# A four-layer megakernel: the order of all engines' steps written out anew

## What is computed

```python
x = L0_attn_x
xn = _layernorm(x, axis=-1)
s = _L0_attn_ref(xn, ...)          # rotary + Mamba-2 style chunked state space mixer
g = _silu(_L0_ffn_ref(xn, ...))    # gated MLP, inputs and weights quantized to FP4 in blocks of 16
x = x + s * g
xn = _layernorm(x, axis=-1)
s = _L1_attn_ref(xn, ...)          # attention over 16 heads within a token, 1.5-entmax by sorting
g = _silu(_L1_ffn_ref(xn, ...))    # mixture of 8 experts, top 2
x = x + s * g
xn = _layernorm(x, axis=-1)
s = _L2_attn_ref(xn, ...)          # gated delta rule: a recurrence over all tokens, rotated state
g = _silu(_L2_ffn_ref(xn, ...))    # mixture of 8 experts, top 2, with a shared expert
x = x + s * g
xn = _layernorm(x, axis=-1)
s = _L3_attn_ref(xn, ...)          # causal attention, 16 heads, relative positions by a skew
g = _silu(_L3_ffn_ref(xn, ...))    # gated MLP, integer weights
x = x + s * g
```

## Time and profile before

| | us |
|---|---|
| median of three runs | 3212.63 |
| the three runs | 3210.42, 3212.63, 3227.47 |
| span of the profiled execution | 3209.0 |
| layers 0 to 2, with the loads ahead of them | 0 to 1951 |
| layer 2's outputs | 1951 to 2233 |
| layer 3: preparation, attention, feed-forward | 2233 to 2300, to 3110, to 3209 |
| table loads on ACT | 94 |

### The profile page before, as it was taken

The page is one execution under the profiler, slowest core; times in us unless marked ns, Lnnn a source line. Parts: engine busy times, 40 slices in busy tenths (PEclk is TensorE's granted clock), DMA queues, the critical chain, the costliest instruction groups (busy, mean ns, idle before and its releaser), DMA issues.

```text
span 3209.0 us, 40003 instructions
## 1 busy us (share of the span) xinstructions
PE 2383.4 (74%) x13729; PEld 1300.2 (41%) x13729; DVE 2544.2 (79%) x5554; ACT 1633.2 (51%) x3182; POOL 565.8 (18%) x610
## 2 busy tenths in 40 slices
PE   3697876967958769679674304997688898888888
PEld 1333333333333333334331101332366676666663
DVE  3386898998999999989989673887577777777764
ACT  1344436245344353353442412666587888777862
POOL 0000300302203003012030020001332323323320
PEclk9698987977978879779777655999799999999999
DMA  2001100100101001001010004200688877888751
GB/s 73 1 22 43 30 25 28 35 32 23 34 29 30 26 24 33 28 27 31 30 24 23 23 8 123 57 9 31 198 226 223 235 222 225 220 215 227 220 157 43
DMA packets 270758, 265.92 MB, mean 83 GB/s; under 512 B 15224, under 2 KB 244235, under 8 KB 268987
## 3 DMA queue, kind: packets, MB, share of 16 engines
q1 hardware_dynamic: 270554, 263.37, 28.8%
HBM read 130.48 MB, written 124.45 MB: 79 GB/s over the span
## 4 chain that ended last, share of the span: by engine, by line
DVE 41%; PE 31%; ACT 14%; issue 9%; DMA 2%; POOL 2%; SPq 1%; DVEq 0%; POOLq 0%; ACTq 0%
PE banks L2642 5%; PE banks L2688 4%; DVE t L2618 3%; DVE t L1017 2%; PE banks L2602 2%; DVE t L1169 2%; ACT L144 2%; DVE t L952 1%; ACT t L2629 1%; PE banks L1085 1%; ACT t L2553 1%; DVE t L2673 1%; DVE t L1700 1%; DVE t L1704 1%; ACT t L1395 1%
## 5 line engine op out<-in xcount | busy, mean ns | idle before, releaser
L2618 DVE CUSTOM_DVE_ANT_0 t<-banks,t 128x640 f32<-128x640 f32 (+7 forms) x512 | 377.8, 747 | 135.2 <-PE banks L2642 62.2
L2629 ACT ACTIVATE t<-t 128x640 f32<-128x640 f32 (+7 forms) x512 | 391.0, 780 | 81.3 <-DVE t L2618 80.4
L2642 PE MATMUL banks<-ident,t 128*128 128x128 f32 x2304 | 360.1, 281 | 41.6 <-DVE t L2839 14.4
L2642 PEld LDWEIGHTS banks<-ident,t 128*128 128x128 f32 x2304 | 253.8, 142 | 108.1 <-ACT t L2629 50.5
L2602 PE MATMUL banks<-t 128*128 128x512 bf16 (+3 forms) x768 | 197.3, 333 | 39.4 <-DVE t L2618 37.5
L2583 POOL TENSOR_TENSOR t<-t 128x512 f32<-128x512 f32 x96 | 122.6, 1277 | 551.1 <-DMA t<-relative_scratch 455.7
L548 POOL TENSOR_TENSOR t<-t 128x512 f32<-128x512 f32 x28 | 48.1, 1718 | 915.7 <-ACT t L520 915.7
L2673 DVE COPY t<-banks 128x512 f32<-128x512 f32 x256 | 175.6, 686 | 32.2 <-PE banks L2642 31.3
L1085 PE MATMUL banks<-t 128*128 128x512 f32 x256 | 145.0, 650 | 42.9 <-DVE t L1165 32.3
L1740 ACT ACTIVATE t<-t 128x16 f32<-128x16 f32 x256 | 82.5, 322 | 184.1 <-DVE t L1704 142.4
L1119 ACT ACTIVATE t<-banks 128x512 f32<-128x512 f32 x128 | 76.4, 597 | 195.6 <-PE banks L1085 195.4
(11 more groups left out here) (453 smaller groups left out, 5956.2 us busy)
## 6 DMA issues: line engine op xcount, KB each, us to landing
relative_scratch<-t SPq DMA_DIRECT2D x128, 512.0 KB, 3.6
t<-relative_scratch SPq DMA_DIRECT2D x128, 512.0 KB, 5.2
relative_scratch<-t SPq DMA_DIRECT2D x128, 256.0 KB, 4.1
t<-in_wmoe SPq DMA_DIRECT2D x64, 384.0 KB, 3.0
t<-cut_scratch SPq DMA_DIRECT2D x192, 64.0 KB
t<-t SPq DMA_DIRECT2D x16, 512.0 KB, 4.2
cut_scratch<-t SPq DMA_DIRECT2D x8, 768.0 KB, 4.1
z_scratch<-t SPq DMA_DIRECT2D x8, 512.0 KB, 3.1
```

The lines of the kernel that those rows point to most:

```text
L2618: nc.vector.tensor_tensor_reduce(s.s[z][:, 0:n], ps[:, b0:b0 + 1 + i // 4, :].rearrange("p b n -> p (b n)")[:, 0:n], s.bias[r][:, j, WIDE ...
L2629: nc.scalar.activation(s.s[z][:, 0:n], s.s[z][:, 0:n], ACT.Exp, scale=-1.0, bias=s.least[:, z:z + 1]).then_inc(*a.mark("weights", u))
L2642: nc.tensor.transpose(ps[:, 4 + c % 2, (t - lo) * P:(t - lo + 1) * P], s.s[u % NS][:, t * P:(t + 1) * P], k.ident[:]).then_inc(*e.mark("tu ...
```

## The change

Ten strings of letters are replaced, nothing else. Each new string has the same number of each letter as the old one (TURNS_SP has one q less, which issued nothing). So every part issues its instructions in its own order as before; what differs is which part's step stands next to which on an engine. The new strings of layers 0 to 2 don't repeat from round to round, and those of the attention don't either. The core of the diff (lines of 112 letters):

```diff
 TURNS_PE = (
...
-    "ammmmmmmiimimmiimmiimmmmmmimimimimmmmeeettttttettmegegmaeeaeeeeaeeeeaeeeaefeeeeeemeeeemfefffeffeffeefeemeeemeeee"
...
+    "miiiimmmmmimmmmmmiimmimmmmmmmmttmmmmmttmteemtteetmgegeaaeaeeaeaeefmeeeefeffeefeeffeeffeeefeeeeffffeefeeeeeeeebee"
...
 )
 TURNS_ACT = (
...
-    "meeetttttgtgtgteggekmkmmeaeaeeaaefemeemfffffeemameeffeemmamaffmmefiebebaammmmrmmrarrirrimirimrmriirriririirrirrr"
...
+    "mmeetttttetteggtgggemkekmmaeaaeafmmmmeffeffffffffiebaeeeeemmaaeemeaaemmemmmbammmiiiiiiiiiimmimiiiirrriririririir"
...
 )
 TURNS_DVE = (
...
-    "afaafafefararaeafaefarafarfeffarfafafefefafefafeffefafafmefmafefmefmafmrrmamrmeiarbeebabararrmammamamramrarmrmra"
...
-    "rrrrrrrrrrrrrrrrrrrrrrrrrrrrrrrrrrrrrrrrrrrrrrrrrrrrrrrrrrrrrrrrrrrrrrrrrrrrrrrrrririririririiiiigiiiigigggggggg"
...
+    "afeeaafffffffffffffffffffffeaeeaaiaaeaeaeaaeaaeaeaeaaeeaaeamreeraaaaaraaaaaaaammrrrmmrmmmrrrmrrmmmrmmrrrmrrrrmmm"
...
+    "rrrrrrrrrrrrrrrrrrrrrrrrrrrrrrrrrrrrrrrrrrrrrrrrrrrrrrrrrrrrrrrrrrrrrrrrrrrrrrrrrrrrrrrrrrrrrrrriiirrrrggggggggg"
...
 )
 TURNS_SP = (
-    "bwtixqxwwqxxqqwwwwwwwwxxiiitqtwwwwwwwwxxiiittqwwwwwwwwbxxiiittqwwwwwwwwbxxiiittqqwwwwwwwwbxxiiittwwwwwwwwbxiiitt"
...
+    "twixbqqwwxxxqqwwwwwwwwxxiiittqwwwwwwwwxxiiittqwwwwwwwwbxxiiittqwwwwwwwwbxxiiittqwwwwwwwwbxxiiittwwwwwwwwbxiiittw"
...
 )
 TURNS3_DVE = (
-    "rabrrrrrrrrrrrrraaaabababababbbrrbaarbabrrrrrbrarararbrbbaaaabbbbaaababbbaaababbbaaababbbaaababbbaaababbbaababba"
...
+    "arbrrrrrrrrrrrrrbbbbbbbbaaaaaaababrbrbbaarbarrrrrbaababbraaababbbaaababbbaaabbabbraaababbbaaababbbaaababbraarabr"
...
 )
 TURNS4_PE = (
-    "vtsvssvvvvvvsttsssttssttttstvttsvtsvttsvsstvtsstvttsttvttsvvtstvtssstvtsstvtttvsttvttvsstvtstsstvsttsvttsvttvtsv"
...
+    "vstvvvssvvvvsttsssttsstttstttvttsstvtsvttssvvsstvttsttvttsvtvsttvssstvtssttvttsvttvtstvsttsvttsvsttvssttsvttvtst"
...
 )
 TURNS4_DVE = (
-    "vtsssstststststssvtvsstsvtvstststssvtvsstststvsvtstsstvvstsststvsvtststvsvsststvsvtststsstvsvstststvsvtstsstsvtv"
...
+    "vtsssstststststsstsvvtstsvvstststssvtvsstststvsvtstsstsvvtstssvtsvtstsstsvvtstsststsvvtsstsstvvstststvvssttssstv"
...
 )
```

More of the change, by code:

```diff
@@ L1821 @@
[L1821 to L1822 removed]
+    "aigefmbtmmmfmmfmffmffmffmffmmffmmmmmmffmmmmfmmmmmmmmmmmmmmmmmmeememaeaamaafeeeeeeeeefeeeffeeeeeeeefeemeeeeeeemee"
+    "eemffeffefeeeemeeeemeeeemmeffeemmmmmmmmffmmfeeeaaeeeaemmmmmmmmammiiimmmmmmmmiiiimmmmmmmmimmimimmimmmeemettetttte"
+    "tteeemgegeeeaaeaeaeaeeeefmffffffffffffffeeeeeeemeeeemeeemeeeeemeemeeeeeeeeeeaeeeeeeeaeeemmeaammmmmmmmmmiiimmmmmm"
@@ new lines @@
+    "mmbmammiiiriiririrmrmriimrmimmirmrrririrrirmiririrrirerirrrrrrrrrrreeiimmgggttttggtgttggtekkemammaaeaefffefffeff"
+    "fffieebeeaemmmaameeaaeeeemmememmrrrrrrrrmrmrmrbarimririirmrmrrrriirmmririririmirrrririririmmiimmiiiimmgggmmemmee"
+    "ggtttttegttggtekmkeaeaaafmmeeffefffemmffmmffmmfimemaebmeeaameeaaemebmeeeaiiiiiimiiiiimiimiiiiiiriimgmrrrrrrrrrrr"
+    "rrrrrrrrrrrrrrrrrrrrggmmmmmmmttggtttegteeggttikekeaaaeaebeeeeeeeeeeaeeeaabeaaeaiiiiiiiiiiiiiirirririrririrrrrrrr"
+    "rrrrrrrrrrrrrrrrrrgggiittttggtgtggttkkbbrrrrrrrrrrrrrrrrrrrrrrrrrrrrrrrrbb"
@@ new lines @@
+    "efmaeaeeaaaeaeaeaaaaeaaaaeeaaeafaafaefaeffffffaaeaaafeefmmfammammmfeffffffmfffffmmmeemmaaaeaemaammmaammeiamiimmm"
+    "immiiiiiimmmiimimgiimimmiimegggeeeeeeggeeeeggggggegggggggmgfggmemererrrraaeaaafffffffffaafafeaafafffffffffffffff"
+    "ffffffaaeaaaemaeeaaaaaeaaaeeaaiareraaeaeaammreraeeaeaeemmaeaeemammaamarrmmmarmmrrrmiirrrrrrrrrrrrrrrrrrrrmiimmrr"
+    "rrrrmmiiirrrrrrriimrrrrrrrrrrrrrrrrrrrrarrrrrrrrrrrrrmmrrrrrrrrrrmrrrmmrrrrrrirrrrirrrrrrrrrrrrrrrrrrrrirrriirrr"
+    "rrrrrrrrrrrrrrrrrrrrrrrrrmiiimmrrrrmrrrrmggmmmggggggggggmgggggegggmeeeeeefggeeeemmrerrraeaeaeafffffffffeaefeaafe"
@@ new lines @@
+    "rrrrrrrrrrrrrrrrrrrrrrrrrrrrrrrrrrrrrrrrrrrrrrrrrrrrrrrrrrrrrrrrrrrrrrrrrrrrrrmrrmmmrrrrregggggggggggeeegggggmmg"
+    "ggeeggefmeeeemrrrrraaaeafffffffffeaefeafafemaeefffffffffffffffffffffeaaaaeeaaiaeaaeeaaaaaemmaeemmbaeaaeemammarer"
+    "eemaaeammaemammrrrraamaammmrmmbarmrrmaraarbrmmrmmraarmrrrrimimrrrrrrrrrrrrrrraerrrrrrrmirriiiiiirrmrrrrrrrrrrrrr"
+    "rrrrrrrrmrirrrrrrrrrrrmrrrirrrrrmrrrirmrrrrrrrrgrrrrrrriirrrrrrrrrrrrrrrrrrrrrrrrrrrrrrrrrrrrrrrrrrrrriiirrrgrrr"
+    "rggggggggggemegggggegggeeeeggmfeeeemrrrrraeaaeafffffffffeeafafafeafffffffffffffffffffffaeaeaaiaaeaaeeaaeaeaeamaa"
@@ new lines @@
+    "stsvtssvstvtstvsststvsstvstsvtstvstssvtssvststvtsvsttssvtssvtststvstvsstsvtsssvttstvtvsssvtstsvstvsvtstvststsvts"
+    "svstststvtssvtsstvsvststvststvsststsvtssvstvtsvtsstsvtssvtstsvtstvstssvtssvtststvstsvtsstsvtsvsstvtsvstsvtsststv"
+    "stsvtvstsstvtsssvtsvtsvtsvtsstsvtssvtststvstsvststvsvststvststvsststsvtssvstsvtvststsvtssvtststvstvsstsvtssvtsts"
+    "tvstsvtsstvsvsstvtststssvtstsvtssvststvtsvtsstsvtsvststvstvstssvststvststvssvtstvstsvststvststssvtstsvtssvstvsts"
+    "vtstsvststsstvststvsttssvtsststsvsttsstsvtv"
@@ L2742 @@
+    "svvstststststvvsstsstsvvtstststvvstssstvvstststvvststssstvvstststvvstsstsvvtstsstststvvsstsstvvstststvvststsssts"
+    "tvvststvvststsvsstvststvsvtststvvvv"
 )
```

151 lines of the change are left out of this document (64 added, 87 removed).

## The result

The changed kernel takes 3400.06 us (median of 4 runs, 3391.45 to 3405.92) against 3220.05 us (4 runs, 3210.42 to 3227.82): ratio 1.0568, 95% interval 1.0531 to 1.0604. It is 5.7% or some 180 us slower. I had said slower, 3289 us, range 3217 to 3352; the time lies 48 us outside that range.

What follows compares the result with a forecast made beforehand. It took VectorE (DVE) as busiest, 79% of the span and 93% from 400 to 1650 us. Terms 72 + 20 - 22 + 2 + 4 = +76 us on the profiled 3209.0 gave 3285, as runs' median 3289 us; range 3217 to 3352.

Steps and rivals of the forecast that it cites:

- (a): DVE in layers 0 to 2: 725 more instructions directly behind one they need, 0.114 us each; 72 us, bounds 66 to 83.
- the early ones: 96 of the 725 new dependent neighbours, in the first 300 us of DVE work; half charged, as DVE idles there.
- Rival one: The flush is paid anyway, or extra neighbours fall into existing waits, so they cost nothing; 3217 us, chance 0.09.
- (b): ACT in layers 0 to 2: 30 more table loads and tighter chains that DVE waits for; 20 us, bounds 0 and 88.
- tighter chains: Less DVE work between chain ends at mixer, in2 and experts, each 2 to 4 us tighter per round; within 20 us.
- (c): Behind layer 1's last update: 24.4 us more recurrence work left to this idle stretch; gain 22 us, bounds 0 and 24.4.
- Rival three: Tighter chains add up: (b) at its bound of 88, (a) at 83; 3368 us, chance 0.11 for over 3335.
- The block and the fillers: End of the stage: 107 recurrence letters (28 us) ahead of the last three in2 steps, 9 to 12 in idle gaps.
- (d): Layer 2's outputs: 38 more dependent neighbours, 4.3 us on DVE, half charged; 2 us, bounds 0 and 4.3.
- (e): Layer 3's attention: 101 more dependent DVE neighbours, 11.5 us, a third charged; 4 us, bounds -94 and +94.
- L280 to L304 0.03 us behind each other: Sign for (a): these DVE instructions start 0.03 us behind each other instead of overlapping a stranger.
- no 8.22 us gap: Sign for (c): the old order's 8.22 us DVE idle between the L1345 at the stage's end disappears.

Runs made afterwards that it cites:

- neighbours_quiet: Old order, layers 0 to 2's DVE string: successors pulled up at most three places, only past instructions no other engine waits for; 3247.0 us, 1.0089.
- neighbours_loud: Old order, layers 0 to 2's DVE string: successors pulled up at most three places, only past instructions another engine waits for; 3342.6 us, 1.0388.
- neighbours_down: Old order, layers 0 to 2's DVE string: instructions no other engine waits for put off at most three places, to just ahead of their successors; 3423.4 us, 1.0644.
- outputs_early_readout: Old kernel with the new sequence of the halves in layer 2's outputs, but the readout's steps as far along as before; 3243.9 us, 1.0090.
- new_order_best_dve: Changed kernel with only the DVE string of layers 0 to 2 laid anew, freely; PE, ACT and SP keep the changed order; 3371.3 us, 1.0487.
- better_order: Old kernel with another PE, ACT, DVE and SP order in layers 0 to 2, found by replaying measured durations; 3224.2 us, 1.0022.
- better_dve_order: Old kernel with only layers 0 to 2's DVE string changed, so that work stands ahead of waits; 3197.1 us, 0.9948.

## Why the prediction was right in sign and wrong in size

The sum was 72 + 20 - 22 + 2 + 4 = 76 us. Measured against it:

(a) **Dependent neighbours, 72: right mechanism, slightly too small.** Small gaps grew by 91.2 us, over my upper bound of 83. Of these, about 80 are neighbours as I priced them: 695 more instructions start 0.01 to 0.06 us behind the one ahead (mean 0.034), each in place of a start 0.081 us before its end. The other 11 are short waits and overlap lost to waits. Five more kernels give 0.09 to 0.11 us of small gaps per neighbour, and the half that I took off the early ones was not due. In whole time neighbours_quiet gives 29 us for 372, 0.08 each. Rival one is refuted, and with it the Trainium skill's rule that a flush follows every DVE op (VectorE: DVE Perf Modes, "The DRAIN you can't avoid"), taken as I took it, whatever comes next: neighbours_quiet changes only who stands behind whom, past instructions that no other engine waits for, and is 29 us slower. The same page's remark that an instruction which isn't held starts earlier agrees with the L1169 above.

(b) **Loads and tighter chains, 20: the step that failed.** The waits grew by 80 us in the account, four times the term; since the account covers the end of the stage too, where (c)'s 8 us were won, it is some 88 us ahead of that end. The loads' share, which I took at half of 39 us, is about 22 and was well sized; what I set at nothing beside them, the tighter chains, is the rest, some 58 us. The prediction says "I take 20 us for loads and tighter chains together, about half of the loads", and names the mixer's L603, the L1345 and L1169 as 2 to 4 us tighter per round. Of these L1169 and L603 came true (5.1 to 32.1 and 8.5 to 16.7 us); L1345 didn't grow (14.1 and 14.1 up to the last L1027); L615 and L760, that I hadn't looked at, gave 36 us more. Rival three, the chains add up, had 88 us for this and was the right case, at 0.11, though its own sum, 3368, is still 32 us short.

For L1169 the reason is not that PE is slower: the experts' three products together have 492.8 us of records after and 496.1 before. I take it to be the distance between a request and its wait. I measured that in means over a round, which hides the short ones, and the new rounds, from 198 to 278 us, are far from equal; by the count under the neighbours the pairs of L1169 with little between them hold 9 us of it, the first L1169 of the units 18. For L615 and L760 slower products are a rival that no run excludes: the mixer's PE records add up to 676 us instead of 644, layer 0's quantized part to 150 instead of 131, and all PE records of the stage to 1984 instead of 1932. neighbours_loud and neighbours_down, with 93 and 129 us of waits from moves of at most three places, show how sharply the old order fitted its chains, in 215 us rounds that all look alike. The durations, for which the sum had no term, grew by 9.

(c) **End of the stage, -22: a third of it came.** From L1027 to L1545 the kernel before shows

```profile
1761.40:1842.50 81.10, 32.45 (x88) 15.74 (x88) 52.01 (x162) 33.94 (x77) 0.00 (x0) 0.63 0.07 23
```

and after stands as the second row of the stretches above. 24.2 us of DVE work moved behind L1027 (76.2 against 52.0 busy), just as counted; but the stretch grew by 16 us, from 81.1 to 97.1, where I had 1. The block and the fillers took away only 8 of 29 us of idle: the L1345 waits went from 14.9 to 2.5, in one place, and new ones came at L1704, 5.2 us behind ACT. So -8 instead of -22.

(d) **Outputs, +2: mis-sized**, 14 us (9 to 20). I priced 38 neighbours and nothing else; it is the sequence of the halves, as far as outputs_early_readout tells. Why exactly stays open.

(e) **Attention, +4: nothing measurable**, 1 us (-4 to +5), inside my bounds.

What I had named as signs: rounds of 226 to 235 us (mean 233.9), 124 loads (124), L280 to L304 0.03 us behind each other (yes), no 8.22 us gap (the longest at L1345 is 3.0), attention within 20 us (yes). Longer waits at L1345 were named too and didn't come. The sign "I am wrong if a wait of several us per round appears at one line" came true: L1169 waits 32 us in eight units.

What stays open: the changed PE and ACT order itself, and how the waits divide into missing cover and slower products. new_order_best_dve leaves some 155 us of loss with the best DVE string that I found. No run takes the changed string of one engine alone, and which of their moves costs what isn't settled.

## What to carry to other kernels

In a hand-written order of several engines the bill had two parts here. One is countable ahead: each DVE instruction that needs the one directly ahead costs about 0.1 us. The other, the waits on other engines, was as large, and means over a round didn't tell it: moving DVE instructions by at most three places cost 0.9% when they passed only instructions that no other engine waits for, and 4 to 6% when they passed others. One place to look is, for every wait, how much own work lies between the request and the wait, the shortest of them first; for L1169 that found a quarter of the wait in the changed kernel and half of it in neighbours_down. And a reckoning that lays measured durations end to end ranks orders near the old one (it gave 2094 us for the changed stage, measured 2132) but over-promises for orders found by it, 85 us said and 7 lost. It holds durations fixed, and two of them moved with the order: PE's products with its granted clock, and L611 with GpSimd's L548. Look at those before a gain or a loss is put down to cover.

## What the hardware showed

With less work on PE its granted clock fell in both orders: with the experts' columns halved it went from 0.83 to 0.76 in the old order (PE busy 1277 and 1185 us up to the last update) and from 0.78 to 0.73 in the new one. A product of 512 columns took 1.13 us for both of its pieces at a granted clock of 1.00, and 2.05 at 0.50, behind 2.5 us of idle PE (better_order). A DVE product of 128x256 (L611) took 0.41 us by itself and 1.48 when it started while GpSimd was in its product L548, ending 0.28 us behind it: 25 of 25 times in the kernel before, 4 of 8 in better_dve_order.
